# Expert mixture behind a graph layer, one core: the scales move behind the down product, are spread by DMA, and Pool adds the experts up

## The chip, the cores and the metric

The kernel runs on one core of one Trainium2 chip. The metric is the device time of one execution in microseconds (us); lower is better. Before the change the median of 3 runs is 1698.33 us (1698.3 to 1698.5).

## What is computed

There are 10,000 tokens (N) of 128 features (D) and an adjacency matrix of 10,000 x 10,000. The reference, cut to what matters:

```python
h = item_feat @ W_item.T + b_item                       # 10000 x 128
b = layernorm(x) @ W_user.T + b_user
x = x + relu(adj @ h + b)
xf = layernorm(x)
probs = softmax(xf @ gate_w + gate_b)                   # 8 experts
cw = top-2 entries of probs, all others zero            # 10000 x 8
for e in range(8):                                      # every expert on every token
    y = gelu(xf @ W1[e] + b1[e]) @ W2[e] + b2[e]        # 128 -> 256 -> 128
    out = out + cw[:, e] * y
x = x + out
```

## The kernel before

**Tiling.** The tokens go in NB = 20 blocks of T = 500, which lie along the free dimension; features lie on the partitions. For a block, `adj @ h` is a sum over 10,000 items: 78 tiles of 128 items and a rest of 16 (`KREM`). A block is walked in NPOS = 40 *positions*: 39 positions of CT = 2 tiles and one, the last (`p == NC`), with the 16 remaining items. The matrices are fp32, and a product is made of three fp32r matmuls: every operand is split in a high part (rounded by a copy) and a low part (the difference), and the kernel adds hi x hi, hi x lo and lo x hi (lines 760 to 762). So a position has 6 matmuls of 128 x 500 on TensorE (PE), one copy on ScalarE (ACT, L391, writes `a_hi`), one subtraction on VectorE (DVE, L543, writes `a_lo`) and one load of 500 KB from SyncE's queue (SP, L304). `a_hi` has 4 buffers, so ACT and DVE can be at most 4 positions ahead of PE; `raw` has 8, so loads can be 8 ahead.

**Order by hand.** Every engine walks the same 40 positions, and constants (`T_*`, `U_*` for PE, `A_*` for ACT, `V_*` for DVE, `STARTS`, `DOWN`) say at which position an engine does each other step. While block i's adjacency product runs, the *tail* of the block before it is done (ReLU L415, residual L598, transposes L801, layernorm L563 to L577, transposes back L768, gate product L810, softmax and top-2 L614 to L653), and then its experts, which run on into the next block (`experts(i - 1, p + NPOS)`). Pool (GpSimd) does nothing but two powers of -0.5 on 125 x 4 elements a block (L348, L352).

**An expert before.** At `STARTS[e]` PE makes z (6 matmuls, L833 to L835) and spreads the token weights of expert e over 128 partitions by a matmul with a 0/1 matrix (L843, into `ps_w`). ACT applies gelu (L456); DVE multiplies by `ps_w` (L671); for experts 0 to 5 ACT copies the high part (L465) and DVE subtracts (L680), and PE makes 6 fp32r matmuls into `ps_y` (L786 to L788). Experts 6 and 7 aren't split: their down product is a plain fp32 matmul, which the hardware runs as two instructions (L792). All experts accumulate in the one bank `ps_y`, begun by two matmuls that add the bias b2 weighted by the scales (L853, L854). DVE adds the residual (L687) from a copy that ACT makes (L438), and ACT stores the block (L470). After the last block's adjacency product there are its tail, the rest of block 19's experts and all eight of block 20's, without adjacency work beside them.

The last position before, and the code of the spreading matmul:

```python
tiles = CT if p < NC else 1
...
nc.tensor.matmul(ps_w[:, 0:T], pick_sb[:, e * P:(e + 1) * P], cw_parts[:, :], start=True,
                 stop=True).then_inc(spread_done, 1)
```

Of the kernel before, what the change touches and what calls it, by code (L numbers as in the profile page):

```python
# [85 lines left out]
AHEAD = 2  # L86
A_RELU, A_TOKEN, A_NORM, A_EXP, A_SPLIT, A_SPREAD, A_STORE, A_KEEP, A_USER, A_FFN, A_SCALED = 2, 5, 12, 17, 25, 26, 31, 37, 38, 4, 6
V_X1, V_STATS, V_NORM, V_LO, V_FINISH, V_USTATS, V_UNORM, V_FFN, V_SCALED = 2, 7, 9, 25, 29, 12, 34, 4, 7
V_LOGITS, V_PROB, V_COMPARE, V_RANK, V_WEIGHT, V_SPREAD = 16, 18, 20, 21, 22, 26

def build(nc, adj_main, adj_rem, xT, xR, itemT, item_rem, w_itemT, b_item, w_userT, b_user, gate_w,
          gate_b_rows, w1, b1, w2, b2, ident, before, pick, outT):
# [6 lines left out]
    with ExitStack() as ctx:  # L101
# [19 lines left out]
        w_item_sb = sb("w_item_sb", [P, D])  # L121
# [20 lines left out]
        x1_kept = sb("x1_kept", [P, T])  # L142
# [28 lines left out]
        gs_hi = [[sb(f"gs_hi{s}_{j}", [P, T], fp32r) for j in range(HH)] for s in range(2)]  # L171
        gs_sb = [sb(f"gs_sb{j}", [P, T]) for j in range(HH)]
        gs_lo = [sb(f"gs_lo{j}", [P, T], fp32r) for j in range(HH)]

        o_sb = r_sb
# [24 lines left out]
        w2_landed = [sem(f"w2_landed{n}") for n in range(-(-NSPLIT * HH * D // T))]  # L200
# [20 lines left out]
        xt_ready = sem("xt_ready")  # L221
# [717 lines left out]
```

## Time and profile before

| | before |
|---|---|
| median of 3 runs | 1698.33 us |
| profiled execution | 1698.34 us |
| its span | 1696.5 us |
| PE busy | 1668.4 us (98%), 7485 matmul instructions |
| DVE busy | 1464.3 us (86%) |
| ACT busy | 1230.0 us (72%) |
| POOL busy | 68.4 us (4%) |
| DMA, mean over the span | 250 GB/s |
| granted TensorE clock | 0.998 of 2.4 GHz |

The profiled execution took as long as the median. The span leaves out 1.8 us that lie around it. "Busy" is the time in which an engine had at least one instruction running; matmuls overlap one another, so that the duration of one isn't the time it costs in a dense row. The page's groups give, for each line, the busy time, the mean duration and the idle time just before.

### The profile page before, as it was taken

What the parts mean: (1) busy time and instruction counts of PE and PEld (TensorE: products, weight loads), DVE (VectorE), ACT (ScalarE), POOL (GpSimd) and SP (SyncE); (2) the same over time, 40 slices, a digit from 0 to 9 for tenths busy, and PEclk for the clock granted to TensorE, in tenths of its full rate; (3) what the DMA queues carried; (4) which work ended last, traced back from release to release, by engine and by line L of the source; (5) the groups of instructions that cost most, each with busy time, mean ns of one, the idle gap of its engine ahead of it and who ended that gap; (6) DMA issues with size and microseconds to landing.
All of it is one profiled execution on the core that took longest, in us unless ns stands there. A gap on an engine that the chain in (4) does not pass through costs nothing.

```text
span 1696.5 us, 26827 instructions
## 1 busy us (share of the span) xinstructions
PE 1668.4 (98%) x7485; PEld 1354.0 (80%) x7485; DVE 1464.3 (86%) x2285; ACT 1230.0 (72%) x1596; POOL 68.4 (4%) x63
## 2 busy tenths in 40 slices
PE   7999999999999999999999999999999999999997
PEld 6878888888888888887878787888888888888864
DVE  5988989898888888888889898989898989898864
ACT  4778777777777677777777777767777777777764
POOL 1000000000000000000000000000000000000000
PEclk9999999999999999999999999999999999999999
DMA  9998777787877787777778787777777777777700
GB/s 358 331 334 286 246 265 249 254 252 261 250 256 254 254 252 259 250 257 248 254 240 268 247 265 254 255 251 252 260 249 266 249 254 254 258 251 258 253 24 13
DMA packets 124639, 423.73 MB, mean 250 GB/s; under 512 B 14262, under 2 KB 19895, under 8 KB 124619
## 3 DMA queue, kind: packets, MB, share of 16 engines
q1 hardware_dynamic: 120456, 415.41, 74.7%
q10 hardware_dynamic: 3314, 5.71, 0.9%
q0 software_dynamic: 848, 2.36, 0.4%
q8 instruction: 10, 0.16, 0.0%
q14 instruction: 11, 0.08, 0.0%
HBM read 418.31 MB, written 5.12 MB: 250 GB/s over the span
## 4 chain that ended last, share of the span: by engine, by line
PE 95%; DVE 2%; DMA 1%; ACT 1%; issue 0%; SPq 0%; ACTq 0%; DVEq 0%
PE acc L760 21%; PE acc L762 21%; PE acc L761 21%; PE ps_z L833 4%; PE ps_z L834 4%; PE ps_z L835 4%; PE ps_y L792 4%; PE ps_y L786 3%; PE ps_y L788 3%; PE ps_y L787 3%; PE ps_w L843 2%; PE acc L778 1%; PE ps_x L768 1%; PE ps_g L810 1%; DMA raw<-in_adj_main 1%; DVE gs_lo L680 1%
## 5 line engine op out<-in xcount | busy, mean ns | idle before, releaser
L543 DVE TENSOR_TENSOR a_lo<-raw,a_hi 128x1000 fp32r<-128x1000 f32 (+1 forms) x800 | 930.2, 1184 | 130.7 <-ACT a_hi L391 128.6
L391 ACT ACTIVATE a_hi<-raw 128x1000 fp32r<-128x1000 f32 (+1 forms) x800 | 800.3, 1025 | 213.4 <-PE acc L762 198.3
L760 PE MATMUL acc<-a_hi,h_hi 128*128 128x500 f32 x1580 | 644.6, 408 | 4.4 <-DVE a_lo L543 3.5
L762 PE MATMUL acc<-a_hi,h_lo 128*128 128x500 f32 x1580 | 614.5, 389 | 0.0
L761 PE MATMUL acc<-a_lo,h_hi 128*128 128x500 f32 x1580 | 613.3, 388 | 0.0
L760 PEld LDWEIGHTS acc<-a_hi,h_hi 128*128 128x128 f32 x1580 | 297.2, 188 | 73.5 <-issue 18.7
L761 PEld LDWEIGHTS acc<-a_lo,h_hi 128*128 128x128 f32 x1580 | 297.8, 188 | 67.6 <-issue 12.8
L762 PEld LDWEIGHTS acc<-a_hi,h_lo 128*128 128x128 f32 x1580 | 297.2, 188 | 60.3
L456 ACT ACTIVATE g_sb<-ps_z,b_sb 128x500 f32<-128x500 f32 x320 | 199.1, 673 | 96.0 <-DVE gs_lo L680 89.7
L680 DVE TENSOR_TENSOR gs_lo<-g_sb,gs_hi 128x500 fp32r<-128x500 f32 x240 | 151.9, 675 | 40.5 <-PE ps_y L788 39.3
L671 DVE TENSOR_TENSOR g_sb<-ps_w,g_sb 128x500 f32<-128x500 f32 x240 | 151.2, 672 | 7.5 <-ACT g_sb L456 7.5
L465 ACT ACTIVATE gs_hi<-g_sb 128x500 fp32r<-128x500 f32 x240 | 134.9, 613 | 2.9 <-DVE g_sb L671 2.9
L833 PE MATMUL ps_z<-xn_hi,w_hi 128*128 128x500 f32 x320 | 125.8, 393 | 8.7 <-ACT g_sb L456 8.7
L834 PE MATMUL ps_z<-xn_lo,w_hi 128*128 128x500 f32 x320 | 125.0, 391 | 0.0
L835 PE MATMUL ps_z<-xn_hi,w_lo 128*128 128x500 f32 x320 | 124.5, 389 | 0.0
L786 PE MATMUL ps_y<-gs_hi,w_hi 128*128 128x500 f32 x240 | 94.6, 394 | 1.1 <-DVE gs_lo L680 1.1
L788 PE MATMUL ps_y<-gs_hi,w_lo 128*128 128x500 f32 x240 | 93.2, 388 | 0.0
L787 PE MATMUL ps_y<-gs_lo,w_hi 128*128 128x500 f32 x240 | 93.0, 387 | 0.0
L352 POOL TENSOR_TENSOR rstd_sb<-var_sb,power_sb 125x4 f32<-125x4 f32 x20 | 37.3, 1867 | 1363.5 <-DVE var_sb L572 1363.5
L833 PEld LDWEIGHTS ps_z<-xn_hi,w_hi 128*128 128x128 f32 x320 | 60.3, 188 | 25.1 <-ACT g_sb L456 13.0
L792 PE MATMUL ps_y<-gs_sb,w_sb 128*128 128x500 f32 x160 | 74.2, 586 | 1.2 <-DVE gs_sb L671 1.2
L671 DVE TENSOR_TENSOR gs_sb<-ps_w,g_sb 128x500 f32<-128x500 f32 x80 | 50.6, 674 | 27.1 <-PE ps_y L792 24.9
(121 smaller groups left out, 1058.5 us busy)
## 6 DMA issues: line engine op xcount, KB each, us to landing
raw<-in_adj_main SPq DMA_DIRECT2D x780, 500.0 KB, 4.6
xr_sb<-in_xR SPq DMA_DIRECT2D x20, 250.0 KB
x_sb<-in_xT SPq DMA_DIRECT2D x20, 250.0 KB, 3.7
out<-r_sb ACTq DMA_DIRECT2D x20, 250.0 KB, 5.1
items<-in_itemT SPq DMA_DIRECT2D x13, 384.0 KB, 8.4
g_sb<-in_w POOLq DMA_DIRECT2D x4, 250.0 KB, 7.4
raw<-in_adj_rem SPq DMA_DIRECT2D x20, 31.2 KB, 3.8
r_sb<-in_w POOLq DMA_DIRECT2D x2, 250.0 KB, 7.8
```

The source lines that it names most:

```text
L391: nc.scalar.activation(a_hi[q][0:rows, 0:cols], raw[s][0:rows, 0:cols], ACT.Copy).then_inc(hi_ready, 1)
L456: nc.scalar.activation(g_sb[j][:, :], ps_z[j][:, 0:T], ACT.Gelu, bias=b1_sb[:, e * HH + j:e * HH + j + 1]).then_inc(gelu_ready, 1)
L543: nc.vector.tensor_tensor(a_lo[s][0:rows, 0:cols], raw[s][0:rows, 0:cols], val(a_hi[q][0:rows, 0:cols]), ALU.subtract).then_inc(lo_ready, 1)
L671: nc.vector.tensor_tensor(scaled[:, :], ps_w[:, 0:T], g_sb[j][:, :], ALU.mult).then_inc(gs_ready, 1)
L680: nc.vector.tensor_tensor(gs_lo[j][:, :], g_sb[j][:, :], val(gs_hi[e % 2][j][:, :]), ALU.subtract).then_inc(gs_lo_ready, 1)
L760: nc.tensor.matmul(acc[:, 0:T], w_hi, m_hi, start=(k == 0), stop=False)
L761: nc.tensor.matmul(acc[:, 0:T], w_hi, m_lo, start=False, stop=False)
L762: last = nc.tensor.matmul(acc[:, 0:T], w_lo, m_hi, start=False, stop=(k == KT))
L786: nc.tensor.matmul(ps_y[:, 0:T], w2_hi[:, cols], gs_hi[e % 2][j][:, :], start=False, stop=False)
L833: nc.tensor.matmul(ps_z[j][:, 0:T], w1_hi[:, at:at + P], xn_hi[:, :], start=True, stop=False)
L834: nc.tensor.matmul(ps_z[j][:, 0:T], w1_hi[:, at:at + P], xn_lo[:, :], start=False, stop=False)
L835: nc.tensor.matmul(ps_z[j][:, 0:T], w1_lo[:, at:at + P], xn_hi[:, :], start=False, stop=True).then_inc(z_done, 1)
```

## The change

1. **Scales behind the down product.** `L671` (gelu times scale), `L843` (spreading matmul), `L853/L854` (bias matmuls), `L656`, `L687` and `L438` go. Every expert has its own down product in one of two banks `ps_y` (four in the last block: the two, `acc` and `ps_x`). DVE then does `t = (y + b2[e]) * spread`, one instruction of 128 x 500 an expert, and Pool adds `t` to `o_sb`.
2. **Spreading by DMA.** The scales of a block stay as 8 rows `cwT_sb`; SP issues for each expert one DMA that reads row e, which lies in one partition, 128 times and writes 128 partitions (4 buffers `spread_sb`).
3. **All 8 experts are split**: experts 6 and 7 now have the high and low parts and 6 fp32r matmuls.
4. **The last 16 items take one product.** The host lays the 16 rows three times (rows 0, 32, 64 of 80); hi, lo and the low part of h are arranged so that one matmul makes the three products.
5. **Tail and order.** The layernorm reads the transposed residual from PSUM (no copy L418); `xn_hi` and `xn_lo` are made straight from PSUM, so that z no longer waits for the gate; experts start at position 14 instead of 27, every 5 positions; the down product stands 8 positions behind. The constants of the first block (`pick`) go, and with them a wait of the eighth `raw` load.

```diff
-STARTS = (27, 31, 35, 39, 44, 49, 54, 59)
-NSPLIT = 6
-DOWN = [8 if e < NSPLIT else 6 for e in range(E)]
+STARTS = tuple(range(14, 14 + 5 * E, 5))
+DOWNS = tuple(p + 8 for p in STARTS)
+SCALES = (32, 34, 37, 40, 45, 50, 55, 60)
+ADDS = tuple(p + 1 for p in SCALES)
+LAST_SCALES = (37, 38, 42, 43, 47, 52, 57, 60)
+SPREADS = 4
+S_SPREAD = (34, 34, 34, 35, 40, 45, 49, 54)
-T_TURN, T_BACK, T_GATE, T_TRANS = 2, 10, 13, 23
+T_TURN, T_BACK, T_GATE, T_TRANS = 2, 9, 14, 23
+A_RELU, A_NORM, A_XN, A_EXP, A_SPREAD, A_STORE, A_USER, A_FFN, A_SCALED = 2, 11, 13, 17, 26, 30, 38, 4, 6
+P_TAIL, P_USER = 6, 14
...
+            def spread(i, p):
+                for e in range(E):
+                    if p != S_SPREAD[e]:
+                        continue
+                    if e == 0:
+                        sp.wait_ge(cwT_ready, i)
+                    since(sp, scaled, expert(i, e) - (SPREADS - 1))
+                    sp.dma_start(spread_sb[e % SPREADS][:, :],
+                                 cwT_sb[e:e + 1, :].unsqueeze(1).to_broadcast([1, P, T])).then_inc(spread_landed[e % SPREADS], 16)
...
+                    pool.wait_ge(scaled, expert(i, e) + 1)
+                    if e == 0:
+                        since(pool, stored, i * 16 - 16)
+                        pool.wait_ge(x1_ready, i)
+                    else:
+                        pool.wait_ge(added, expert(i, e))
+                    nc.gpsimd.tensor_tensor(o_sb[:, :], x1_sb[:, :] if e == 0 else o_sb[:, :], t_sb[e % 2][:, :],
+                                            ALU.add).then_inc(added, 1)
...
-                if p == A_TOKEN:
-                    nc.scalar.activation(xt_sb[0:TQ, :], ps_v[0:TQ, :], ACT.Copy).then_inc(xt_ready, 1)
                 if p == A_NORM:
                     act.wait_ge(t_back, i)
+                    nc.scalar.activation(xn_hi[:, :], ps_x[:, 0:T], ACT.Copy).then_inc(xn_hi_ready, 1)
+                if p == A_XN:
+                    act.wait_ge(xn_lo_ready, i)
                     nc.scalar.activation(xn_sb[:, :], ps_x[:, 0:T], ACT.Copy).then_inc(xn_ready, 1)
...
-                        nc.vector.tensor_tensor(scaled[:, :], ps_w[:, 0:T], g_sb[j][:, :],
-                                                ALU.mult).then_inc(gs_ready, 1)
+                    dve.wait_ge(down_done, expert(i, e) + 1)
+                    dve.wait_ge(spread_landed[e % SPREADS], i * (16 * E // SPREADS) + 16 * (e // SPREADS + 1 - E // SPREADS))
+                    since(dve, added, expert(i, e) - 1)
+                    nc.vector.scalar_tensor_tensor(out=t_sb[e % 2][:, :], in0=y[:, 0:T], scalar=b2_sb[:, e:e + 1],
+                                                   in1=spread_sb[e % SPREADS][:, :], op0=ALU.add,
+                                                   op1=ALU.mult).then_inc(scaled, 1)
...
-                tiles = CT if p < NC else 1
+                if p == NC:
+                    nc.tensor.matmul(acc[:, 0:T], h_hi[:, KT * D:(KT + 1) * D], a_hi[q][:, 0:T],
+                                     start=False, stop=True).then_inc(adj_used, 1)
+                    return
...
             def down(i, e):
+                since(pe, scaled, expert(i, e) - (len(banks) - 1))
                 for j in range(HH):
+                    pe.wait_ge(g_lo_ready, i * (E * HH) + (HH * (e - E) + j + 1))
+                    nc.tensor.matmul(y, w2_hi[:, cols], hi, start=(j == 0), stop=False)
+                    nc.tensor.matmul(y, w2_hi[:, cols], lo, start=False, stop=False)
+                    last = nc.tensor.matmul(y, w2_lo[:, cols], hi, start=False, stop=(j == HH - 1))
...
-                    nc.tensor.matmul(ps_w[:, 0:T], pick_sb[:, e * P:(e + 1) * P], cw_parts[:, :], start=True,
-                                     stop=True).then_inc(spread_done, 1)
-                        nc.tensor.matmul(ps_y[:, 0:T], b2_hi[:, :], cw_parts[:, :], start=True, stop=False)
-                        nc.tensor.matmul(ps_y[:, 0:T], b2_lo[:, :], cw_parts[:, :], start=False, stop=False)
```

## Rows read from the trace of the kernel before

**Rows 1.** Window of one block: length; busy PE, PEld, DVE, ACT, POOL; clock; DMA share; GB/s.

```profile
826.84:908.50 81.66, 81.66 (x367) 66.45 (x366) 72.10 (x113) 60.58 (x79) 2.92 (x2) 1.00 0.79 255
```

**Rows 2.** The chain that ended last, shares of the span by engine.

```profile
PE 95%; DVE 2%; DMA 1%; ACT 1%; issue 0%; SPq 0%; ACTq 0%; DVEq 0%
```

**Rows 3.** PE's timeline: start, duration; fp32 matmuls between fp32r, then fp32r alone.

```profile
1600.20 0.38 PE L762 MATMUL acc<-a_hi,h_lo 128*128 128x500 f32 x1
...
1600.43 1.84 PE L792 MATMUL ps_y<-gs_sb,w_sb 128*128 128x500 f32 x4
...
1602.33 0.39 PE L761 MATMUL acc<-a_lo,h_hi 128*128 128x500 f32 x1
...
1624.04 0.38 PE L760 MATMUL acc<-a_hi,h_hi 128*128 128x500 f32 x1
1624.27 0.39 PE L761 MATMUL acc<-a_lo,h_hi 128*128 128x500 f32 x1
1624.49 0.39 PE L762 MATMUL acc<-a_hi,h_lo 128*128 128x500 f32 x1
```

**Rows 4.** Groups by line: busy us, mean ns, idle before and releaser.

```profile
L671 DVE TENSOR_TENSOR g_sb<-ps_w,g_sb 128x500 f32<-128x500 f32 x240 | 151.2, 672 | 7.5 <-ACT g_sb L456 7.5
L465 ACT ACTIVATE gs_hi<-g_sb 128x500 fp32r<-128x500 f32 x240 | 134.9, 613 | 2.9 <-DVE g_sb L671 2.9
...
L656 DVE TENSOR_TENSOR cw_parts<-ps_g,cw_parts 8x500 fp32r<-8x500 f32 x20 | 13.4, 669 | 0.6
```

**Rows 5.** DVE's timeline: start, us, two subtractions of `gs_lo` in a row.

```profile
904.64 1.26 DVE L680 TENSOR_TENSOR gs_lo<-g_sb,gs_hi 128x500 fp32r<-128x500 f32 x2
```

**Rows 6.** Pool's two powers: in block 12, its neighbour on DVE, at the end.

```profile
908.50 1.91 POOL L352 TENSOR_TENSOR rstd_sb<-var_sb,power_sb 125x4 f32<-125x4 f32 x1 [70.31 <-DVE var_sb L572]
908.35 1.20 DVE L543 TENSOR_TENSOR a_lo<-raw,a_hi 128x1000 fp32r<-128x1000 f32 x1
1637.84 1.01 POOL L352 TENSOR_TENSOR rstd_sb<-var_sb,power_sb 125x4 f32<-125x4 f32 x1 [64.64 <-DVE var_sb L572]
```

**Rows 7.** ACT's timeline in block 11's tail: exp between its two table loads.

```profile
843.85 1.28 ACT L430 ACT_TABLE_LOAD   x1
845.14 0.23 ACT L430 ACTIVATE exp_sb<-shift_sb 125x32 f32<-125x32 f32 x1
...
846.32 1.28 ACT L456 ACT_TABLE_LOAD   x1
```

**Rows 8.** DMA: bytes of one block; the GB/s of 800 to 830; issues to landing.

```profile
DMA packets 6074, 20.79 MB, mean 255 GB/s; under 512 B 680, under 2 KB 952, under 8 KB 6074
...
GB/s 277 320 144 293 325 384 192 0 0 19 35 186 336 274 280 373 400 411 421 421 357 139 112 160 363 379 240 336 421 384 320 368 160 171 325 101 91 240 341 117
...
x_sb<-in_xT SPq DMA_DIRECT2D x1, 250.0 KB, 3.9
```

**Rows 9.** The start: the chain's step, then PE's first product that waits for it.

```profile
1.72 7.89 DMA raw<-in_pick
...
10.12 0.69 PE L740 MATMUL ps_v<-cw_parts,pick_sb 128*128 128x384 f32 x1 [2.80 <-DVE pick_sb L524]
...
19.42 13.53 DMA raw<-in_adj_main
```

**Rows 10.** The end: last adjacency matmul, block 20's first gelu, two z, store issue.

```profile
1628.07 0.39 PE L762 MATMUL acc<-a_hi,h_lo 128*128 128x500 f32 x1
...
1657.17 1.25 ACT L456 ACTIVATE g_sb<-ps_z,b_sb 128x500 f32<-128x500 f32 x2 [2.93 <-DVE r_sb L687]
...
1679.36 0.49 PE L833 MATMUL ps_z<-xn_hi,w_hi 128*128 128x500 f32 x1 [0.25 <-ACT g_sb L456]
1682.95 0.49 PE L833 MATMUL ps_z<-xn_hi,w_hi 128*128 128x500 f32 x1 [0.24 <-ACT g_sb L456]
...
1693.59 0.35 ACTq L470 DMA_DIRECT2D out<-r_sb  x1
```

More of the change, by code:

```diff
@@ L163, in build @@
         cw_sb = sb("cw_sb", [TQ, Q * E])
-        cw_parts = sb("cw_parts", [P, T], fp32r)
-        g_sb = [sb(f"g_sb{j}", [P, T]) for j in range(HH)]
+        cwT_sb = sb("cwT_sb", [E, T])
+        with ExitStack() as whole:
+            g_sb = [[whole.enter_context(nc.sbuf_tensor(f"g_sb{s}_{j}", [P, T], fp32)) for j in range(HH)] for s in range(2)]
+        g_lo = [[sb(f"g_lo{s}_{j}", [P, T], fp32r) for j in range(HH)] for s in range(2)]
         with ExitStack() as first_pass:
             items = [first_pass.enter_context(nc.sbuf_tensor(f"items{s}", [P, 2 * GD], fp32)) for s in range(ISLOTS)]
[L171 to L175, printed above, removed]
+            w_item_sb = first_pass.enter_context(nc.sbuf_tensor("w_item_sb", [P, D], fp32))
+            ones_sb = first_pass.enter_context(nc.sbuf_tensor("ones_sb", [P, P], fp32r))
+            bias_rows = first_pass.enter_context(nc.sbuf_tensor("bias_rows", [P, GD], fp32r))
+        g_hi = [[sb(f"g_hi{s}_{j}", [P, T], fp32r) for j in range(HH)] for s in range(2)]
+        spread_sb = [sb(f"spread_sb{s}", [P, T]) for s in range(SPREADS)]
+        t_sb = [sb(f"t_sb{s}", [P, T]) for s in range(2)]
         gt_sb = xt_sb[0:TQ, 0:Q * E * E]
@@ L333, in _ @@
                         load_x(i)
+                    if with_finish:
+                        spread(i - 1, p + NPOS)
+                    spread(i, p)
+            one_pass(1, False)
+            with sp.Fori(2, NB) as i:
+                one_pass(i, True)
+            for p in range(NPOS):
+                spread(NB - 1, p + NPOS)
+                spread(NB, p)
+            for p in range(NPOS, 2 * NPOS):
+                spread(NB, p)
         @block.gpsimd
@@ L430, in tail @@
                     nc.scalar.activation(exp_sb[:, :], shift_sb[:, :], ACT.Exp).then_inc(exp_ready, 1)
-                if p == A_KEEP:
-                    if not (isinstance(i, int) and i == 1):
-                        act.wait_ge(out_ready, i - 1)
-                        act.wait_ge(stored, i * 16 - 16)
-                    act.wait_ge(x1_ready, i)
-                    nc.scalar.activation(x1_kept[:, :], x1_sb[:, :], ACT.Copy).then_inc(kept_ready, 1)
                 if p == A_SPREAD:
                     act.wait_ge(cwT_done, i)
-                    nc.scalar.activation(cw_parts[0:E, :], ps_g[0:E, 0:T], ACT.Copy).then_inc(cw_hi_ready, 1)
+                    since(act, scaled, expert(i, 0))
+                    nc.scalar.activation(cwT_sb[:, :], ps_g[0:E, 0:T], ACT.Copy).then_inc(cwT_ready, 1)
             def experts(i, p):
@@ L541, in split_lo @@
                 dve.wait_ge(hi_ready, i * NPOS + (p + 1))
-                rows, cols = (P, CT * T) if p < NC else (KREM, T)
-                nc.vector.tensor_tensor(a_lo[s][0:rows, 0:cols], raw[s][0:rows, 0:cols],
-                                        val(a_hi[q][0:rows, 0:cols]), ALU.subtract).then_inc(lo_ready, 1)
+                whole, high = raw[s][:, :], a_hi[q][:, :]
+                low = a_lo[s][:, :]
+                if p == NC:
+                    whole, high = (t[LO_ROW:LO_ROW + KREM, 0:T] for t in (raw[s], a_hi[q]))
+                    low = high
+                nc.vector.tensor_tensor(low, whole, val(high), ALU.subtract).then_inc(lo_ready, 1)
             def weights(p):
@@ L774, in user @@
                     pe.wait_ge(u_normed, i + 1)
+                    since(pe, xn_ready, i)
                     back(xr_sb, u_turned)
```

277 lines of the change are left out of this document (118 added, 159 removed).

## The prediction

> **What bounds the kernel now.** I read the chain of waits first, then a window of one block, then the timelines. The chain lies on PE for 95% of the span [rows 2], so time is what PE's instruction stream takes. One block of the steady part, from one `rstd` on Pool to the next, is 81.66 us, and PE is busy in all of it, at full clock (granted clock 1.00, the 2.4 GHz level) [rows 1]. DVE has 72.10 us and ACT 60.58, so 9.56 and 21.1 us of slack; the DMA engines are busy for 0.79 of the block [rows 1]. A change pays if it takes instructions from PE, and only until DVE, ACT or DMA fills the block.
>
> The reader is to see one trap here. The timeline gives an fp32r matmul of 128 x 500 a duration of 0.39 us, but the next one starts 0.23 us after it (1624.04, 1624.27, 1624.49) [rows 3]: durations overlap. 0.45 us for two steps is 0.225; with the longer rows around them I take 0.227. That is the price of a matmul on the path, not 0.39. A plain fp32 product costs more: between the start of L762 at 1600.20 and L761 at 1602.33 lie 2.13 us for L762, four L792 and L760; less 2 x 0.227, the four cost 1.68, 0.42 each [rows 3].
>
> **The change part by part, per block.**
>
> PE loses 8 spreading matmuls and 2 bias matmuls: 10 x 0.227 = 2.27 us. Experts 6 and 7 had 8 fp32 instructions, 8 x 0.42 = 3.36, and get 12 fp32r, 12 x 0.227 = 2.72: 0.64 less. The last position has 1 matmul for 3: 0.45 less. All of it stood on the path, since PE has no idle time in the block. The new period would be 81.66 - 2.27 - 0.64 - 0.45 = 78.30 us.
>
> DVE loses 16 multiplications (L671), `cw_parts` (L656) and the output add (L687), about 0.67 each [rows 4]. A pair of 128 x 500 in a row takes 1.26 us [rows 5], 0.63 each: 16 x 0.63 + 0.67 + 0.67 = 11.4 less. It gains four `g_lo`, 4 x 0.63 = 2.5, and eight scale operations. No such three-operand form of 128 x 500 from PSUM is in the trace; its nearest row is L671, which also reads PSUM and SBUF, 0.67 us [rows 4]; bounds 0.6 to 1.0. 8 x 0.67 = 5.4. DVE goes to 72.1 - 11.4 + 2.5 + 5.4 = 68.6 us, hidden under PE with 9.7 us left. If it weren't, each us over would be a us a block.
>
> ACT loses two copies of 0.6 us (L418, L438) and gets four high-part copies, 0.61 [rows 4]: 61.8 us of 78.3. But its order matters. The exp of the tail and its two table loads hold ACT for 3.75 us (843.85 to 847.60) [rows 7], and now the gate product (position 14, was 13), the gelu of old expert 7, xn and the first new gelu (18) crowd round them. Following PE from its transposes back at position 9 to `a_lo` of position 19, I find ACT and DVE less than 0.5 us ahead of PE there. Bounds: 0 (there was no idle time before) to 1.5 us a block. I take 0.3.
>
> Pool goes from two small operations to ten. The trace has no Pool add of 128 x 500; the nearest rows are the two-input operation on DVE, 0.67 us [rows 4], and Pool's own operation on 4 elements, 1.01 to 1.91 us [rows 6]. I take 1.3, midway; 8 x 1.3 = 10.4 us of 78.3, so Pool itself is idle enough, and each add has a spacing of 2 to 5 positions of 1.96 us (78.3 / 40) before the second next scale needs its buffer. What it does to DVE is the question. The power on Pool lasts 1.91 us when it starts at 908.50 within a DVE subtraction of two SBUF inputs (908.35 to 909.55), and 1.01 at the end with DVE on other work [rows 6]: it seems to wait for the 1.05 us that DVE still needs, so the two share something, and the other way round an add could hold a DVE instruction. Cost to DVE: 0 to 8 x 1.91 = 15.3 us a block. I take half of 10.4, 5.2, since DVE has idle time and operations with one SBUF input; that fits in 9.7. The Trainium skill, SBUF — State Buffer, section "Who interferes with whom", has it as a rule: a VectorE instruction with two SBUF inputs and a GpSimd one that reads SBUF exclude each other for the whole instruction; the trace agrees on Pool's side, no run yet shows DVE's. Its GPSIMD Engine Reference, section 3.1, gives 4497 ns for an add of 2048 elements; scaled to 500, an estimate of 1.1 us, all eight would hold DVE for 8.8 us, and the sum would still be PE's.
>
> DMA gains eight spreads of 256 KB a block and 128 KB more in the last load. In front of them: SP issues spreads in line with the loads, so a spread that waits for `cwT_ready` or `scaled` holds the next loads. Spread 0 stands behind load 34, which itself waits until PE has done position 26; ACT has made `cwT` at position 26, at most a position later, and loads have 7 positions (13.7 us) of lead. Its waits on `scaled` are met 7 or more positions early. The transfers: lower bound that of a 250 KB load, 3.9 us to landing [rows 8], with some 0.6 us of the engines at the best rate seen, 421 GB/s [rows 8]. Upper bound 9.7 us: if one partition could serve all 16 engines only at the rate at which one of them moves, 421 / 16 = 26.3 GB/s. Nothing in this trace reads one partition many times. I take the lower end for the sum: then the block moves 20.8 + 2.2 MB, 55 us at 421 GB/s, hidden under 78.3. The upper end is rival 2.
>
> New waits: DVE's scale e waits for down e, which PE has at 3 positions less from expert 2 on (10 and 7 for experts 0 and 1). Queued behind it is `a_lo` of the next position; PE then still has 3 positions, 4.1 us, and a scale and an `a_lo` take 1.9: no stall. PE's down e waits for scale e-2; tightest is down 2 at position 32 with scale 0 at DVE's 32, which DVE reaches ahead of PE as long as spread 0 has landed, 10 us after its issue. ACT's gelu waits for the down two experts back, 6 positions behind it: past. Pool's add 0 waits for the store of the last block, 3 positions after its issue (5.9 us; the scale buffer leaves it 8 us more).
>
> **Ends.** Start: PE's first product is held until 10.12 by the `pick` load [rows 9], but the chain soon after lies on an adjacency load of 13.5 us [rows 9]; of the 2.8 us I count 2, bounds 0 to 5. At the turn to the last block, experts that started at 14 instead of 27 have put 24 more matmuls of block 19 ahead of the last adjacency product, less 6 spreading and bias ones: 18 x 0.227 = 4.1 us more there.
>
> The end: the last adjacency matmul ends at 1628.45 and the span at 1696.5, 68.05 us [rows 10]. Block 20's first gelu is at 1657.17 [rows 10], after the gate, the top-2 and the rest of block 19's experts. Now z needs only `xn_hi`/`xn_lo`, and block 19 leaves 36 matmuls. Adding up relu, x1, transposes, statistics, power, normalise, back, xn, gate, exp and the loads between them, I get that gelu 16.4 us after the last adjacency matmul, 28.7 before: 12.3 earlier. Experts then went at 3.59 us each (1679.36, 1682.95) [rows 10], a loop over PE, ACT, DVE, ACT, DVE. The new loop is bound by PE's 12 matmuls, 2.72, or by ACT's 2.4: I take 2.9. That and a last chain of 9.6 (gelu and copy 2.4, `g_lo` 0.7, down 0.9, scale 0.7, add 1.3, wakes 0.7, issue and store 2.9, from 1693.59 to 1696.5 [rows 10]) is 7 x 2.9 + 9.6 = 29.9, was 39.3: 9.4 less. Together 21.7; I take 20, bounds 10 to 26 (DVE has 1.26 + 0.67 + a held 1.3 an expert, 3.2, if every add holds it). The spreads lie beside the first four down products there.
>
> **Sum**, against the profiled execution's 1698.34 us (the median is 1698.33; what lies round the span stays): 18 full blocks of experts x 2.91 = 52.4; last position 20 x 0.45 = 9.0; shift +4.1; stalls 18 x 0.3 = +5.4; start 2; end 20. 1698.34 - 52.4 - 9.0 + 4.1 + 5.4 - 2 - 20 = 1624.4 us.
>
> **Rivals.**
>
> 1. *Pool holds DVE, and DVE becomes the bound.* Each us of delay per add costs DVE 8; from (78.3 - 68.6) / 8 = 1.2 us per add DVE passes PE. At 1.5 us the period is 80.6: 1624.4 + 18 x 2.0 (the 0.3 is in it) = 1660. For it: [rows 6]. Against: DVE's idle time takes part of it. Slower than before it gets only from about 1.8 us per add: 68.6 + 14.1 = 82.7 us, where (82.7 - 78.6) x 18 = 74 eats the whole gain; at 1.91 (83.9 us a block) some 1720.
> 2. *One partition feeds the spread slowly, and DMA becomes the bound*: the rival on the other side. A spread occupies all 16 engines, the loads queue behind it. Free DMA time is 78.3 - 20.8 / 0.421 = 28.9 us, 3.6 us a spread; beyond that every us costs 8 a block. At 9.7 us the block is 49 + 78 = 127 us: 1698 + 19 x 45 - 20 = some 2530 us. For it: all 128 packets read the same 2000 bytes. Against: nothing in the trace but that packets from HBM aren't so bound. The Trainium skill, SBUF — State Buffer, section "Door 1: The DMA port swizzle", says that a partition is reached by one of 16 ports of about 27 GB/s; by that rule a spread takes 9.4 us, an estimate, which is this rival's time; no run here shows it so far.
> 3. *PE's saving turns into waiting* at the crowded positions 14 to 19 (1.5 us a block or more) while the ends gain only 10: 1624.4 + 18 x 1.2 + 10 = 1656; with the whole 3.4 us lost, 18 x 3.1 + 10 = 66 more, 1690. That the matmuls go is certain from the code; that they pay in full isn't.
>
> **How the numbers follow.** Forecast 0.62 (1606 to 1640). Rival 1 with DVE somewhat over, and rival 3, 0.20 together (1640 to 1690), rival 1 to the bad end 0.02, rival 2 0.13, no change 0.02, and 0.01 for faster than 1606. Faster by over 0.2% (3.4 us, about what a measurement of this kernel can tell from no change) is 0.62 + 0.20 + 0.01 = 0.83; within it 0.02; slower 0.15. The range holds the forecast and most of the 0.20: 1606 to 1675. Rival 2 is left out.
>
> **What would show it.** A steady block of 78.3 to 78.6 us with PE busy throughout; DVE near 69 us, more if `a_lo` rows of over 1.2 us stand beside Pool's adds; Pool adds of about 1.3 us; spreads landing in about 4 us and DMA not full. Wrong if `a_hi` waits for `raw` loads (rival 2), if PE waits for `a_lo` in every block (1 or 3), or if the last adjacency matmul ends more than 47 us before the span does.

## The result, and the profile after

The changed kernel takes 2419.12 us (median of 4 runs, 2415.35 to 2421.8), the kernel before 1698.41 beside it: ratio 1.4242, 95% interval 1.4217 to 1.4266. The forecast of 1624.4 us was wrong, range and sign; what happened is rival 2, priced at some 2530 us.

The page of the changed kernel, first part (busy us, share of the span, instructions), and its chain by engine:

```profile
PE 1775.6 (74%) x7325; PEld 1404.2 (58%) x7325; DVE 1548.5 (64%) x2164; ACT 1254.9 (52%) x1637; POOL 318.9 (13%) x223
...
DMA 42%; PE 19%; SPq 16%; issue 9%; DVE 7%; ACT 5%; ACTq 0%; DVEq 0%; POOLq 0%; POOL 0%
```

PE was 95% of the chain [rows 2]; now DMA and the queue that issues loads are 58%. The waits of the same kernel, whole span (engine and tile waited for: us in total, times, longest), say for what:

```profile
ACT a_hi L454 <- DMA raw<-in_adj_main: 842.2, 208, 25.2
...
PE acc L784 <- DVE a_lo L592: 407.5, 132, 15.0
DVE t_sb L710 <- DMA spread_sb<-cwT_sb: 322.2, 42, 15.5
```

ACT waits 842 us for adjacency loads that are late, and PE for what is made of them. It isn't that the loads have grown: HBM was read for 420.34 MB, before for 418.31. One block (columns as in [rows 1]); it is one of the shorter, the 17 full ones have a mean of 116.9 us:

```profile
1094.43:1209.16 114.73, 87.39 (x358) 68.98 (x359) 76.68 (x107) 61.82 (x80) 15.33 (x11) 0.87 0.89 200
```

114.73 us for 81.66, with the DMA engines busy for 0.89 of it (was 0.79) while they move 200 GB/s (was 255): busier, and moving less. The same in slices of 1 us, 1076 to 1116, where the spreads of experts 0 to 3 are issued; the DMA issues of that stretch; SP's queue in it (start, us that the issues took); and a window of 22 us within it:

```profile
DMA  9599999499999499999499999499858968999696
GB/s 220 114 420 284 36 28 30 14 28 30 28 30 30 14 28 30 28 30 28 12 32 28 30 28 28 14 30 30 74 146 302 76 38 26 28 48 40 22 48 120
...
raw<-in_adj_main SPq DMA_DIRECT2D x5, 500.0 KB, 11.8
spread_sb<-cwT_sb SPq DMA_DIRECT2D x4, 250.0 KB, 23.0
...
1075.59 8.50 SPq L344 DMA_DIRECT2D spread_sb<-cwT_sb  x3
1084.33 13.23 SPq L317 DMA_DIRECT2D raw<-in_adj_main  x1
1097.67 8.37 SPq L344 DMA_DIRECT2D spread_sb<-cwT_sb  x1
...
1081.00:1103.00 22.00, 12.61 (x46) 9.71 (x44) 4.51 (x4) 2.62 (x4) 1.99 (x1) 0.77 0.89 26
```

This is the reading of the case: the busy row stands at 9 while most slices of the row under it stand at 28 to 30 GB/s, with every fifth or so at 12 or 14. The mean counts, not the commonest slice: 26 in the window, and 26.6 GB/s in the packet records of the 19 longest stretches in which spreads move alone. All engines are held by packets that come out of one partition. 256,000 bytes at 26.6 GB/s are 9.6 us a spread. The four spreads landed 17.8, 26.9, 30.2 and 19.1 us after their issues, the second 9.7 us behind the first and the fourth 9.7 behind the third. While spreads move alone, their 2000-byte packets take 1.08 us each; in the runs further down that read 128 partitions or HBM, a 2000-byte packet takes 0.08 us (median). The Trainium skill, SBUF — State Buffer, section "Door 1: The DMA port swizzle", gives a port some 27 GB/s; this trace, with 26.6, agrees.

Behind them, SP's queue takes no further issue for 13.23 us (1084.33), and the engines stand still one after the other. ACT, DVE and PE in the same stretch, the idle time ahead of each in brackets:

```profile
1109.19 1.04 ACT L454 ACTIVATE a_hi<-raw 128x1000 fp32r<-128x1000 f32 x1 [25.04 <-DMA raw<-in_adj_main]
...
1093.47 0.74 DVE L710 SCALAR_TENSOR_TENSOR t_sb<-ps_y,b_sb,spread_sb 128x500 f32<-128x500 f32 x1 [11.97 <-DMA spread_sb<-cwT_sb]
...
1094.26 0.78 PE L813 MATMUL ps_y<-g_hi,w_hi 128*128 128x500 f32 x1 [8.47 <-DVE t_sb L710]
...
1094.84 0.62 PE L814 MATMUL ps_y<-g_lo,w_hi 128*128 128x500 f32 x1
1095.26 0.62 PE L815 MATMUL ps_y<-g_hi,w_lo 128*128 128x500 f32 x1
```

PE's stop has a second price. In a window from its first matmul after that stop, and in windows of 8 us around it (columns as in [rows 1]; the clock is the third number from the end), the granted clock reads:

```profile
1094.26:1098.60 4.34, 4.34 (x11) 3.49 (x12) 3.22 (x2) 0.00 (x0) 1.99 (x1) 0.50 0.95 28
...
1078.00:1086.00 8.00, 7.79 (x35) 6.15 (x33) 3.49 (x4) 4.26 (x5) 0.00 (x0) 1.00 0.98 109
1086.00:1094.00 8.00, 0.00 (x0) 0.00 (x0) 0.53 (x1) 0.00 (x0) 0.00 (x0) 0.67 0.92 27
...
1110.00:1118.00 8.00, 3.70 (x10) 2.69 (x10) 1.20 (x1) 1.25 (x3) 0.00 (x0) 0.50 0.88 136
1118.00:1126.00 8.00, 5.50 (x13) 4.45 (x14) 6.73 (x7) 6.92 (x10) 2.15 (x1) 0.50 0.99 248
```

After PE's idle stretch the clock is 0.50, the 1.2 GHz level: an fp32r matmul starts its group with 0.78 us for 0.39, and those behind it stand 0.42 us apart (1094.84, 1095.26) for 0.23. In the block 28 of its 358 matmuls go at that spacing, some 5.3 us. That is the larger part of why PE's busy time grew to 87.39 us though it has nine instructions fewer; for the rest I take the block's nine stops, at each of which a first and a last matmul show their whole duration.

### The profile page after: what moved, and what is told of

It is laid out like the page before. It is cut to its first block, busy times and chain, and to the rows that moved or that the text cites. A ratio compares the mean times of both kernels' runs of the same rounds, so it can differ in the third digit from the quotient of the medians.

```text
span 2413.5 us, 27037 instructions
## 1 busy us (share of the span) xinstructions
PE 1775.6 (74%) x7325; PEld 1404.2 (58%) x7325; DVE 1548.5 (64%) x2164; ACT 1254.9 (52%) x1637; POOL 318.9 (13%) x223
## 3 DMA queue, kind: packets, MB, share of 16 engines
HBM read 420.34 MB, written 5.12 MB: 176 GB/s over the span
## 4 chain that ended last, share of the span: by engine, by line
DMA 42%; PE 19%; SPq 16%; issue 9%; DVE 7%; ACT 5%; ACTq 0%; DVEq 0%; POOLq 0%; POOL 0%
DMA raw<-in_adj_main 24%; DMA spread_sb<-cwT_sb 19%; SPq L317 11%; PE acc L784 5%; SPq L344 4%; PE acc L786 4%; PE acc L785 4%; DVE a_lo L592 3%; ACT a_hi L454 2%; DVE g_lo L701 1%; DVE xt_sb L681 1%; ACT g_sb L502 1%; ACT L502 1%; PE ps_y L813 1%; PE ps_y L814 1%
## 5 line engine op out<-in xcount | busy, mean ns | idle before, releaser
L454 ACT ACTIVATE a_hi<-raw 128x1000 fp32r<-128x1000 f32 (+1 forms) x800 | 804.2, 1025 | 955.3 <-DMA raw<-in_adj_main 842.2
L592 DVE TENSOR_TENSOR a_lo<-raw,a_hi 128x1000 fp32r<-128x1000 f32 x780 | 974.8, 1268 | 477.2 <-ACT a_hi L454 472.5
L405 POOL TENSOR_TENSOR o_sb<-o_sb,t_sb 128x500 f32<-128x500 f32 x140 | 226.3, 1617 | 1031.9 <-DVE t_sb L710 1031.6
L710 DVE SCALAR_TENSOR_TENSOR t_sb<-ps_y,b_sb,spread_sb 128x500 f32<-128x500 f32 x156 | 114.6, 734 | 341.6 <-DMA spread_sb<-cwT_sb 306.8
L813 PE MATMUL ps_y<-g_hi,w_hi 128*128 128x500 f32 x312 | 138.2, 443 | 155.8 <-DVE t_sb L710 115.5
L701 DVE TENSOR_TENSOR g_lo<-g_sb,g_hi 128x500 fp32r<-128x500 f32 x320 | 227.4, 751 | 5.4 <-ACT g_hi L508 5.4
L508 ACT ACTIVATE g_hi<-g_sb 128x500 fp32r<-128x500 f32 x320 | 179.0, 609 | 0.0
L813 PEld LDWEIGHTS ps_y<-g_hi,w_hi 128*128 128x128 f32 x312 | 64.5, 207 | 179.4 <-DVE t_sb L710 154.5
L814 PE MATMUL ps_y<-g_lo,w_hi 128*128 128x500 f32 x312 | 131.7, 422 | 0.0
L815 PE MATMUL ps_y<-g_hi,w_lo 128*128 128x500 f32 x312 | 131.4, 421 | 0.0
L853 PE MATMUL ps_z<-xn_hi,w_hi 128*128 128x500 f32 x320 | 129.3, 404 | 0.0
L854 PE MATMUL ps_z<-xn_lo,w_hi 128*128 128x500 f32 x320 | 125.4, 392 | 0.0
L815 PEld LDWEIGHTS ps_y<-g_hi,w_lo 128*128 128x128 f32 x312 | 65.3, 209 | 14.3
## 6 DMA issues: line engine op xcount, KB each, us to landing
spread_sb<-cwT_sb SPq DMA_DIRECT2D x160, 250.0 KB, 13.8
```

Source lines behind the costliest of these rows:

```text
L405: nc.gpsimd.tensor_tensor(o_sb[:, :], x1_sb[:, :] if e == 0 else o_sb[:, :], t_sb[e % 2][:, :], ALU.add).then_inc(added, 1)
L454: nc.scalar.activation(a_hi[q][0:rows, 0:cols], raw[s][0:rows, 0:cols], ACT.Copy).then_inc(hi_ready, 1)
L508: nc.scalar.activation(g_hi[e % 2][j][:, :], g_sb[e % 2][j][:, :], ACT.Copy).then_inc(g_hi_ready, 1)
L592: nc.vector.tensor_tensor(low, whole, val(high), ALU.subtract).then_inc(lo_ready, 1)
L701: nc.vector.tensor_tensor(g_lo[e % 2][j][:, :], g_sb[e % 2][j][:, :], val(g_hi[e % 2][j][:, :]), ALU.subtract).then_inc(g_lo_ready, 1)
L813: nc.tensor.matmul(y, w2_hi[:, cols], hi, start=(j == 0), stop=False)
```

## The experiments

Two questions: is it the single partition (theory) or the spreads as such, their place in the queue, or the change's other parts (rivals); and why the kernel is still far from 1624 us when the spreads cost little. Ratios are to the kernel before on the same chip, with the 95% interval.

**s128: the same spreads out of 128 partitions.**

```diff
-    sp.dma_start(..., cwT_sb[e:e + 1, :].unsqueeze(1).to_broadcast([1, P, T]))...
+    sp.dma_start(..., val(w1_hi[:, 0:T]))...
```

> The changed kernel with one edit: each spread reads 128 partitions of a constant tile instead of one partition 128 times (same bytes, same count of DMAs, same waits, same places on SP; the scales are left out and replaced by constants). Theory A, one source partition feeds all 16 engines at about 28 GB/s and holds the loads behind it: spreads take under 1 us of the engines, the steady block falls from 114.7 us to 78.3 to 80, the time to 1620 to 1660 us. Theory B, it is the extra 41 MB, the 160 more DMAs or SP's waits in front of the loads: the time stays above 2300 us.

Measured: 1681.49 us, ratio 0.9901 (0.9881 to 0.992). Same bytes, same queue, same places, and 738 us less; a spread lands in 6.0 us (median) for 13.8. The changed kernel's row, then this run's:

```profile
spread_sb<-cwT_sb SPq DMA_DIRECT2D x160, 250.0 KB, 13.8
...
spread_sb<-w_hi SPq DMA_DIRECT2D x160, 250.0 KB, 6.0
```

So the single source partition is the whole slowdown, and neither the number of transfers nor their order is. But the time is above the expected 1620 to 1660 us and 57 us above the forecast.

**onerow: spreads of one row, no fan-out.**

```diff
-    sp.dma_start(spread_sb[e % SPREADS][:, :], cwT_sb[e:e + 1, :]...to_broadcast([1, P, T]))
+    sp.dma_start(spread_sb[e % SPREADS][0:1, :], cwT_sb[e:e + 1, :])
-    in1=spread_sb[e % SPREADS][:, :]
+    in1=val(w1_hi[:, 0:T])
```

> The changed kernel with the spreads cut to a copy of one row of 2000 bytes each; SP keeps its issues and its waits, VectorE scales by a constant tile (the spreading is left out). Theory A: as the run with 128 source partitions, 1620 to 1655 us, at most 1% below it. Theory B by bytes: also near 1625, but then the run with 128 source partitions isn't; theory B by SP's waits: above 2300 us.

Measured: 1676.0 us, 0.9868 (0.9849 to 0.9888): a miss. With no spread traffic at all 52 us are missing, and the 128-partition traffic costs only 5.5 us on top. One block, DVE and Pool in it, and the block's waits:

```profile
794.55:875.75 81.20, 79.32 (x359) 64.63 (x358) 74.44 (x107) 61.98 (x81) 19.18 (x10) 1.00 0.81 257
...
811.27 2.33 DVE L700 TENSOR_TENSOR g_lo<-g_sb,g_hi 128x500 fp32r<-128x500 f32 x2
...
810.40 2.06 POOL L404 TENSOR_TENSOR o_sb<-o_sb,t_sb 128x500 f32<-128x500 f32 x1 [2.75 <-DVE t_sb L709]
...
ACT xn_hi L481 <- PE ps_z L854: 4.3, 1, 4.3
PEld acc L783 <- DVE a_lo L591: 3.4, 4, 2.0
```

PE idles for a_lo, DVE is busy for 74.4 us where I had 68.6, and two causes offer themselves. A pair of subtractions that takes 1.26 us alone [rows 5] takes 2.33 beside an add on Pool, and the add itself 2.06. And ACT stands for 4.3 us before `xn_hi`. The next runs part the two.

**tinyadd: onerow with seven of eight Pool adds cut to 8 columns** (those adds leave out the rest).

```diff
+    wide = T if e == 0 else 8
-    nc.gpsimd.tensor_tensor(o_sb[:, :], ..., t_sb[e % 2][:, :], ALU.add)
+    nc.gpsimd.tensor_tensor(o_sb[:, 0:wide], ..., t_sb[e % 2][:, 0:wide], ALU.add)
```

> The run with one-row spreads (1676 us), with seven of Pool's eight adds cut to 8 of 500 columns (the sum over the experts is left out). Theory L, Pool's adds hold VectorE's operations of two SBUF inputs, and the lateness comes out as PE waits: the block falls from 81.2 to 78.3 to 79.3 us, the time to 1625 to 1640 us. Theory T, the crowded tail alone (gate, exp, table loads at positions 9 to 19) makes the waits: the time stays at 1665 us or more.

Measured: 1645.19 us, 0.9693 (0.9673 to 0.9712), 5 us above the theory's range and 20 below the rival's, a block of 79.94:

```profile
508.77:588.71 79.94, 79.27 (x359) 64.69 (x358) 68.97 (x106) 61.87 (x82) 10.85 (x11) 1.00 0.82 262
```

DVE falls from 74.44 to 68.97 us: the seven adds held it for 5.5 us, near the 5.2 that the prediction gave all eight. But 31 us of the total went with them, so this was not absorbed by DVE's idle time: 18 x 1.26 = 22.7 in the blocks, and 6.6 behind the last relu, from which it is 43.0 us to the end of the span (onerow 49.6).

**halfspread: every second spread has one row only.**

```diff
-    since(sp, scaled, expert(i, e) - (SPREADS - 1))
+    since(sp, scaled, expert(i, e) - (SPREADS - 2))
+    rows = P if e % 2 == 0 else 1
-    sp.dma_start(spread_sb[e % SPREADS][:, :], ...to_broadcast([1, P, T]))
+    sp.dma_start(spread_sb[e % SPREADS][0:rows, :], ...to_broadcast([1, rows, T]))
...
-    in1=spread_sb[e % SPREADS][:, :]
+    in1=spread_sb[e % SPREADS // 2 * 2][:, :]
```

> The changed kernel with every second spread cut to one row, so that 4 spreads of 256 KB a block are left (two experts are scaled by the same row; the scales of experts 1, 3, 5 and 7 are left out). Theory A: a block is 114.7 less 4 x 9.2 = 78 us of DMA time or a little more, about where PE's own 78.3 us end it: 1640 to 1730 us. If the cost of a spread isn't proportional but one wait of the bunch at positions 34 and 35, two spreads there instead of four: above 1800 us.

Measured: 2015.13 us, 1.1865 (1.1837 to 1.1893), far over the theory's range and on the other side, above 1800. One block, its GB/s in 40 slices of 2.4 us, and waits in it:

```profile
841.23:938.07 96.84, 86.02 (x358) 68.34 (x359) 75.98 (x107) 61.63 (x80) 16.26 (x11) 0.93 0.87 225
...
GB/s 28 179 275 358 317 87 70 277 305 287 384 301 325 229 26 26 76 420 420 416 406 380 223 212 220 157 246 278 238 226 274 238 215 235 226 267 90 26 26 29
...
ACT a_hi L455 <- DMA raw<-in_adj_main: 10.7, 5, 4.0
...
PE ps_y L814 <- DVE t_sb L711: 9.4, 2, 6.6
...
DVE t_sb L711 <- DMA spread_sb<-cwT_sb: 6.2, 1, 6.2
```

The expectation took four spreads off a block, 78 us left. By bytes and rate four spreads are 38 us and the rest of the traffic some 49, 88 in all. The block is longer still because the spreads stand in bunches (26 to 29 GB/s twice in the block) with the engines' free time elsewhere: 420 GB/s follows right behind. A scale waits 6.2 us for its spread, PE's down product 9.4 us for the scale two before it, ACT 10.7 us for loads, and the clock falls to 0.93. So half the spreads took 404 us of the 737 away: what a held engine costs depends on who waits at that moment, not on the sum of busy time alone. One thing isn't separated here: two experts share a buffer, so SP waits for one more scale ahead of each spread, with loads behind it. That wait is 13.2 us in this block, 6.4 in the changed kernel's; how much of the 96.84 us it makes no run shows.

**rows16 and rows16c: each scale row laid out 16 times**, so that a spread reads 16 partitions, 8 apart (rows16) or neighbours (rows16c); DVE copies `cw` into that order ahead of the transposes.

```diff
+    nc.vector.tensor_copy(cwr_sb.rearrange("p (q r e) -> p q r e", e=E, r=P // E), ...)
...
-    cwT_sb[e:e + 1, :].unsqueeze(1).to_broadcast([1, P, T])
+    cwT_sb[e:P:E, :].unsqueeze(1).to_broadcast([P // E, E, T])   # rows16c: cwT_sb[e * 16:e * 16 + 16, :]
```

> The changed kernel with the scales laid out 16 times: VectorE copies them to 125 x 512, PE transposes them to 128 rows (row 8r + e is expert e), and a spread reads 16 partitions 8 times each. Nothing is left out. Theory A: what a spread costs falls with the number of sources, to 0.6 us (if each partition has its own 28 GB/s) or about 1.2 us (if 4 or 8 groups of partitions share it): 1625 to 1665 us, faster than before the change (1698). Theory B: above 2300 us.

> As rows16, but the 16 copies of an expert's scales lie in 16 neighbouring partitions (row 16e + r) instead of 8 apart. In rows16 a packet of 2000 bytes had a median of 0.11 us, with 128 sources 0.082, with one 1.08. Theory A1, each partition gives its own 28 GB/s: as rows16, 1690 to 1700 us. Theory A2, groups of partitions share it, and 16 neighbours reach half as many groups as 16 that lie 8 apart: packets of about 0.25 to 0.3 us, 2.2 us a spread, 10 us more DMA a block: 1705 to 1800 us.

Measured: 1695.73 us, 0.9986 (0.9974 to 0.9997), above its range of 1625 to 1665, and 1705.48, 1.0053 (1.0037 to 1.0069), 5 us above the range of theory A1 and at the lower edge of A2's; the packets decide between these two. Spreads land in 7.2 and 6.9 us, a 2000-byte packet takes 0.112 and 0.125 us in the mean, and ACT waits 131.5 and 167.9 us for `raw`. Sixteen sources are nearly as good as 128, wherever they lie; the packets of neighbours are 12% longer, not the 2 to 3 times of a theory in which only distance counts. Their loss against s128 goes with later loads (5.9 and 5.8 us to landing, against 4.7; ACT waits 22.3 us for `raw` in s128); DVE's extra copy, 0.43 us a block, isn't separated from it.

**hbmspread: the scales stored to HBM (16 KB a block) and spread from there.**

```diff
+    act.wait_ge(cwT_ready, i)
+    act.dma_start(kept, cwT_sb[:, :]).then_inc(cwT_kept, 16)
...
-    cwT_sb[e:e + 1, :].unsqueeze(1).to_broadcast([1, P, T])
+    kept[e:e + 1, :].to_broadcast([P, T])
```

> The changed kernel with the 8 x 500 scales stored to HBM by the scalar engine's queue (16 KB a block) and every spread read from there, one row 128 times; nothing is left out. Theory A, only a single SBUF source is slow: 1675 to 1695 us, like the run with 128 source partitions (1681). If reading one address range 128 times is slow wherever it lies: above 1900 us.

Measured: 1681.89 us, 0.991 (0.9893 to 0.9926), with nothing left out. Reading the same 2000 bytes 128 times is harmless in HBM:

```profile
spread_sb<-kept SPq DMA_DIRECT2D x160, 250.0 KB, 6.3
```

So it is not the repeated address but the partition. This version is the base of most of what follows.

**actqueue: the changed kernel, spreads issued by ACT.**

```diff
-    sp.dma_start(spread_sb[e % SPREADS][:, :], cwT_sb[e:e + 1, :]...)
+    act.dma_start(spread_sb[e % SPREADS][:, :], cwT_sb[e:e + 1, :]...)
```

> The changed kernel, but with the eight spreads issued from ScalarE's queue at the same positions, so that SyncE's instruction stream and its queue carry the loads alone; nothing is left out. Theory (one partition feeds all 16 engines, and the engines stand still while they read it): the loads find the same engines taken, so the time stays at 2300 to 2450 us and the wait of a_hi for raw stays. Rival (the loads are late only because they stand behind the spreads in one queue): loads pass the spreads, and the time falls below 1900 us.

Measured: 2457.64 us, 1.4477 (1.4447 to 1.4508); the upper edge of the range was passed by 8 us. Its issues to landing, and its waits:

```profile
raw<-in_adj_main SPq DMA_DIRECT2D x780, 500.0 KB, 8.1
spread_sb<-cwT_sb ACTq DMA_DIRECT2D x160, 250.0 KB, 13.7
...
DVE t_sb L708 <- DMA spread_sb<-cwT_sb: 473.2, 60, 14.5
ACT a_hi L437 <- DMA raw<-in_adj_main: 421.3, 190, 8.8
```

Loads no longer stand behind the spreads (longest wait 8.8 us, was 25.2; 421.3 us in all, was 842.2), but the waits for spreads grow (473.2 us, were 322.2), and it gains nothing: the two queues share engines that are held. A cleverer place in the queues cannot mend this.

**b_rest: the kernel before, with only the rest product (last position) changed**, the layout of its 16 rows with it.

```diff
-    tiles = CT if p < NC else 1
+    if p == NC:
+        nc.tensor.matmul(acc[:, 0:T], h_hi[:, KT * D:(KT + 1) * D], a_hi[q][:, 0:T], start=False, stop=True)
+        return
```

> The kernel before the change with part 4 of it alone, the last 16 items in one product. By the price of 0.227 us a matmul, 40 matmuls fewer give 9.1 us: 1688 to 1690 us. By the duration of 0.39 us they would give 15.5: 1683. If PE's savings are lost to waits: 1698.

Measured: 1687.57 us, 0.9943 (0.9927 to 0.996), 9.9 us below the kernel before beside it (9.1 expected), a block of 81.23 us for 81.66. Two matmuls less a block give 0.43 us: the pitch of 0.227 us [rows 3] is the price of a matmul, not the duration of 0.39. That step of the sum is shown.

**dveadd: hbmspread with the eight adds on DVE**, each a position behind its scale.

```diff
-    nc.gpsimd.tensor_tensor(o_sb[:, :], x1_sb[:, :] if e == 0 else o_sb[:, :], t_sb[e % 2][:, :], ALU.add)
+    nc.vector.tensor_tensor(o_sb[:, :], x1_sb[:, :] if e == 0 else o_sb[:, :], t_sb[e % 2][:, :], ALU.add)
```

> Base: the kernel with the scale rows kept in HBM (hbmspread, 1681.9 us). Here Pool adds nothing: the eight adds of a block stand on VectorE, each one position behind its scale, and nothing is left out. Theory (the adds cost by what they do to VectorE, 1.3 us a block by tinyadd, and two-input operations of 128 x 500 take 0.63 us on VectorE): VectorE's busy time is then about 69 + 8 x 0.63 = 74 us of 80 and no instruction is held; without the lock the block should lie between 79.9 (tinyadd) and 81.4 us and the time between 1650 and 1678. Rival (VectorE is short of time around the crowded positions whoever adds): the block stays at 81.4 us or grows to 82.5 and the time is 1680 to 1705.

Measured: 1659.88 us, 0.978 (0.9764 to 0.9797). 22.0 us faster with eight more instructions of 0.67 us on DVE. DVE's busy time in a block goes from 74.88 (hbmspread) to 73.31: an add that DVE makes itself costs it less than one Pool makes beside it.

```profile
753.44:833.94 80.50, 79.32 (x359) 64.69 (x358) 73.31 (x114) 62.09 (x82) 2.01 (x2) 1.00 0.86 284
```

**start16: hbmspread with experts started two positions later.**

```diff
-STARTS = tuple(range(14, 14 + 5 * E, 5))
-SCALES = (32, 34, 37, 40, 45, 50, 55, 60)
+STARTS = (16, 21, 26, 31, 36, 40, 45, 49)
+SCALES = (32, 34, 37, 42, 47, 51, 56, 60)
```

> Base: the kernel with the scale rows kept in HBM (hbmspread, 1681.9 us, 81.6 us a block). Here the first seven experts start 2, 2, 2, 2, 2, 1 and 1 positions later (STARTS 16, 21, 26, 31, 36, 40, 45, 49), the scales of experts 3 to 6 stand 2, 2, 1 and 1 later; nothing is left out. Theory (PE loses some 1.6 us a block where transposes back, xn, gate, exp and the first gelu crowd positions 14 to 19): with two positions more between them the block falls to about 80.0 to 80.8 us and the time to 1650 to 1670. Rival (the loss is not there but in VectorE held by Pool and in the scales at 32 to 40): the block stays within 0.3 us and the time at 1676 to 1690.

Measured: 1717.49 us, 1.0121 (1.0104 to 1.0138), slower than the kernel before and than its base: both theories missed. One of its longer blocks (they run from 82.7 to 85.6 us, mean 83.4) and its waits:

```profile
776.09:860.20 84.11, 81.31 (x361) 65.74 (x360) 74.48 (x107) 62.37 (x81) 20.71 (x11) 0.99 0.84 272
...
DVE a_lo L596 <- ACT a_hi L456: 6.9, 4, 5.0
...
ACT xn_hi L484 <- PE ps_z L859: 4.9, 1, 4.9
```

Room behind position 14 didn't help, which speaks against experts starting among gate, xn and exp as the trouble. A stall stands earlier: ACT stops for 4.9 us at `xn_hi`, and DVE for 5.0 on ACT's `a_hi`. But the base has the stop at `xn_hi` too, up to 4.9 us, so it doesn't explain the difference. Why this schedule is slower by 36 us than its base stays open.

**norm12: dveadd with `xn_hi` one position later on ACT.**

```diff
-A_RELU, A_NORM, A_XN, ... = 2, 11, 13, ...
+A_RELU, A_NORM, A_XN, ... = 2, 12, 13, ...
```

> Base: dveadd (1659.9 us, 80.5 us a block; scale rows kept in HBM, adds on VectorE). Here ScalarE makes xn_hi one position later (A_NORM 12 for 11); nothing is left out. Theory (ScalarE reaches xn_hi 4.3 us before PE has finished expert 7's z and stands still there, which costs it the lead that the crowded positions 12 to 19 then need; PE loses 1.2 us and more a block to a_lo because of it): the wait falls to 2 to 3 us, PE's waits for a_lo in the block shrink, the block becomes 79.3 to 80.2 us and the time 1635 to 1655. Rival (ScalarE stops there anyway for PE, and its lead is set by a_hi's two buffers): block and time stay within 0.2% of dveadd.

Measured: 1629.82 us, 0.9603 (0.9587 to 0.9619), 30.1 us less for one digit and 5 below the expected range. One block, with its waits; then dveadd's for the same tile, over the whole span, and norm12's:

```profile
738.14:817.09 78.95, 78.81 (x358) 64.87 (x357) 73.44 (x115) 62.19 (x81) 2.92 (x2) 1.00 0.87 290
...
ACT xn_hi L464 <- PE ps_z L849: 2.2, 1, 2.2
```

```profile
ACT xn_hi L464 <- PE ps_z L849: 80.7, 19, 4.3
...
PE acc L778 <- DVE a_lo L576: 26.2, 59, 1.9
```

```profile
ACT xn_hi L464 <- PE ps_z L849: 42.3, 19, 3.0
...
PE acc L778 <- DVE a_lo L576: 4.5, 11, 1.5
```

ACT runs more than two positions ahead of PE. Standing at position 11 it waits for what PE does at position 9 (z of the old block's expert 7, which still reads the old `xn_hi`), and a_hi of 12 waits with it; made behind that a_hi, xn_hi is no later, and ACT keeps the lead: PE's waits for `a_lo` fall from 26.2 us in all to 4.5. PE is busy for 78.81 of 78.95 us again. This kernel leaves nothing out and beats both.

**pooladd12: hbmspread with the same digit changed**, the fourth corner of the square.

> Base: hbmspread (1681.9 us, 81.3 us a block; GpSimd adds). Here only ScalarE makes xn_hi one position later (A_NORM 12 for 11), as norm12 did on the kernel with the adds on VectorE; nothing is left out. Theory (the two causes are independent: the adds held by GpSimd cost 22 us in all by dveadd, the place of xn_hi 30 us by norm12): 1681.9 - 30 = 1652, range 1645 to 1660. Rival (the adds cost time only where the lead is already lost): with the lead kept VectorE's held operations are absorbed, and the time is 1630 to 1640, within 0.6% of norm12.

Measured: 1649.28 us, 0.9719 (0.9703 to 0.9735), inside the theory's range; the rival falls. Two starts of `rstd` in a row give a block of 80.07 us (the mean is 79.8):

```profile
747.15 1.93 POOL L385 TENSOR_TENSOR rstd_sb<-var_sb,power_sb 125x4 f32<-125x4 f32 x1 [2.55 <-DVE var_sb L618]
...
827.22 1.93 POOL L385 TENSOR_TENSOR rstd_sb<-var_sb,power_sb 125x4 f32<-125x4 f32 x1 [2.54 <-DVE var_sb L618]
```

| | adds on Pool | adds on DVE |
|---|---|---|
| `xn_hi` at 11 | 1681.9 | 1659.9 |
| `xn_hi` at 12 | 1649.3 | 1629.8 |

The adds cost 22.0 and 19.5 us, the place of `xn_hi` 32.6 and 30.1: the two add up, to within 2.5 us.

## Why the prediction was wrong, point by point

The account from forecast to measurement, in medians: 1624.4 forecast; 1629.8 the best version that does what the change does (5.4 more); 19.5 for Pool's adds; 32.6 for the place of `xn_hi`; that is 1681.9. Then 737.2 for the single partition: 2419.1. With the spread mended alone the kernel would still have missed the range, which ended at 1675.

- **The spread's price: this step failed.** The text had both ends, 3.9 and 9.7 us, and took the lower "for the sum" though its own row for the lower end is a load out of HBM into many partitions, and the thing to be priced was 128 reads of one. The nearest row was near in bytes and not in the resource that limits. The upper end, one engine's rate of 26.3 GB/s worked out from [rows 8], was right: 26.6 measured, 9.6 us. It rested on an assumption, that one partition serves no more than one engine moves, which no row of the trace before showed and which came true. But with ends that far apart, and the far one carrying 900 us, the near one went into the sum without a row that reads one partition many times.
- **Rival 2's size.** 127 us a block was said, 116.9 measured in the mean. Its sum put full spreads behind full load time; in the trace they overlap in part (around 1105 packets of loads and of a spread move side by side). The mechanism (ACT's `a_hi` waits for `raw`) is as told. It left out PE's clock, 0.87 over the block.
- **Block price of PE: right.** 78.30 forecast with PE busy throughout, 78.95 in norm12. b_rest confirms the pitch for two matmuls of a block; the other parts of the sum weren't run one by one.
- **Stall of 0.3 us a block: wrong by a factor.** It measured 81.20 - 78.30 = 2.9 in onerow. The prediction looked for it at positions 9 to 19 and counted ACT and DVE as half a us ahead of PE, but added up durations only. The stop before `xn_hi` comes from a position number, and the kernel before already had its counterpart, in its block of [rows 1]:

```profile
ACT xn_sb L421 <- PE ps_x L768: 3.7, 1, 3.7
```

  There it cost nothing: PE was busy for all of that block. Rival 3 had a loss of 1.5 us a block, and dveadd against norm12 gives 80.50 - 78.95 = 1.55; but it looked for it at positions 14 to 19, where room didn't help, so that the sizes agree is in part luck.
- **Pool holds DVE: size near, absorption wrong.** 5.2 us a block said for eight adds; seven measured 74.44 - 68.97 = 5.5, so eight some 6.3, an estimate. "That fits in 9.7" compared totals of a block; the delays fall in stretches where DVE has no slack, and 1.26 us a block came out in the period (81.20 - 79.94). The Trainium skill, SBUF — State Buffer, section "Who interferes with whom", has the exclusion both ways; the 2.33 us pair beside a 2.06 us add agrees on DVE's side. A Pool add alone is some 1.25 us (the prediction had 1.3).
- **The scale on DVE:** 0.67 said, 0.73 measured: 0.5 us a block.
- **The end: right.** 20 us said. The last relu follows at once on the last adjacency matmul. From its start to the end of the span the kernel before took 68.0 us (1628.49 to 1696.5); onerow 49.6 (1623.82 to 1673.4), so 18.4 less; norm12 46.6 (1580.94 to 1627.5), so 21.4 less.

## What to carry to other kernels

A DMA that reads one SBUF partition many times holds every DMA engine at that partition's rate; look for "DMA share up, GB/s down" before anything else, and take the source from HBM or lay the row out 16 times. Slack in a block's totals isn't slack at a place: before new work is put into an in-order stream, read for each engine the wait ahead of the step it joins. And when a cost is bounded by two rows far apart, ask which of them uses the same limiting resource, and take that one.

## What the runs showed of the hardware beyond what was expected

- One partition served 26.6 GB/s to all 16 engines together (26.5 in halfspread). With 16 partitions a spread landed in 7.2 and 6.9 us, with 128 in 6.0, and the distance of the 16 mattered little: 0.112 us a packet 8 apart, 0.125 as neighbours.
- The same 2000 bytes read 128 times from HBM cost what distinct bytes cost: 6.3 us to landing, 6.0 from 128 partitions.
- DVE and Pool operations of two SBUF inputs held each other up in both directions: pairs of 1.26 us became 2.33, an add of 1.25 us became 1.99 to 2.16, once a block 3.33. Moving such an add onto DVE (0.67 us) was cheaper for DVE itself.
- PE came back from stops of 8.47, 9.44 and 5.29 us (before 1094.26, 1111.51 and 1120.50) at a granted clock of 0.50; in 1126 to 1134 it read 0.99 again.
